# Up product of the routed expert tiles with the expert's weights as the stationary operand

## The reference

```python
xt = layernorm(x).reshape(2048, 512)
probs = softmax(xt @ W_router)                          # 16 routed experts, each token takes 2
rt_mid = gelu(einsum('th,ehd->ted', xt, Wrt_up))        # 512 -> 256
routed_out = einsum('ted,edh->th', rt_mid * gate, Wrt_down)   # 256 -> 512
```

## Time and profile before

| | us |
|---|---|
| median of three runs | 2106.89 |
| lowest and highest | 2105.78, 2107.63 |
| the profiled execution, its own time | 2111.85 |
| its span, first to last instruction | 2110.2 |
| stage of the routed tiles, first to last gelu start | 267.3 to 441.8 |

### The profile page before, as it was taken

How to read it: one execution, slowest core, us unless ns; L and a number is a source line. 1 busy time by engine, 2 the same in 40 slices (tenths; PEclk the granted TensorE clock), 3 DMA queues, 4 the chain that set the end, 5 groups by cost and what they waited for, 6 DMA issues and landing times. The chain is left out here.

```text
span 2110.2 us, 28970 instructions
## 1 busy us (share of the span) xinstructions
PE 1998.1 (95%) x9797; PEld 1654.6 (78%) x9801; DVE 1324.3 (63%) x2087; ACT 851.0 (40%) x1649; POOL 907.6 (43%) x802
## 2 busy tenths in 40 slices
PE   4989999957999999999999999999979999999999
PEld 4766788845888888887888888888867888888887
DVE  7985688867787676768676666666665333333333
ACT  4543299944444444444444444444432111111111
POOL 1100044434766767766666656666641122201200
PEclk9999999987999999999999999999989999999999
DMA  7350299964765666656555555555520010100002
GB/s 286 125 190 25 91 364 410 410 231 132 203 182 167 178 175 188 184 165 190 146 166 164 165 147 153 158 161 161 170 90 12 30 31 30 31 0 30 0 1 80
DMA packets 133759, 307.18 MB, mean 146 GB/s; under 512 B 15648, under 2 KB 17056, under 8 KB 133664
## 3 DMA queue, kind: packets, MB, share of 16 engines
q1 hardware_dynamic: 113600, 239.35, 36.7%
q0 software_dynamic: 20064, 66.60, 9.4%
HBM read 210.73 MB, written 95.16 MB: 145 GB/s over the span
## 5 line engine op out<-in xcount | busy, mean ns | idle before, releaser
L1482 POOL TENSOR_TENSOR t_pT_lo<-t_pT_raw,t_pT_hi 128x512 fp32r<-128x512 f32 x256 | 327.9, 1301 | 214.6 <-ACT t_pT_hi L1598 213.0
L1708 DVE TENSOR_REDUCE t_sums<-t_score 128x1 f32<-128x512 f32 x256 | 169.4, 687 | 128.8 <-PE t_score L52 128.4
L2084 DVE TENSOR_TENSOR f_lin<-f_lin,f_silu 128x512 f32<-128x512 f32 x64 | 44.7, 699 | 290.6 <-PE f_lin L52 290.6
L1613 ACT ACTIVATE t_probs<-t_score,t_sums 128x512 f32<-128x512 f32 x256 | 174.9, 683 | 84.1 <-DVE t_sums L1708 68.8
L1698 DVE STREAM_TRANSPOSE t_blocks<-t_probs 128x512 f32<-128x512 f32 x256 | 172.6, 693 | 23.9 <-ACT t_probs L1613 23.8
L1690 DVE SCALAR_TENSOR_TENSOR x_res<-t_out,t_sums,x_res 128x512 f32<-128x512 f32 x256 | 179.4, 740 | 7.4 <-PE t_out L52 7.4
L1598 ACT ACTIVATE t_pT_hi<-t_pT_raw 128x512 fp32r<-128x512 f32 x256 | 159.8, 625 | 3.9 <-DMA t_pT_raw<-turned_blocks 3.9
L2045 ACT ACTIVATE f_silu<-f_gate 128x512 f32<-128x512 f32 x64 | 38.3, 598 | 299.4 <-PE f_gate L52 299.4
L1592 ACT ACTIVATE t_o_hi<-t_o 128x512 fp32r<-128x512 f32 x64 | 38.3, 598 | 218.2 <-PE t_o L52 218.2
L1578 ACT ACTIVATE t_k_hi<-t_score 128x512 fp32r<-128x512 f32 x64 | 38.3, 598 | 204.6 <-PE t_score L52 204.6
L52 PE MATMUL t_score<-t_wv_hi,t_cT_hi 128*128 128x256 f32 x416 | 117.8, 283 | 0.8 <-ACT t_probs L1613 0.7
(11 more groups left out here) (351 smaller groups left out, 5953.0 us busy)
## 6 DMA issues: line engine op xcount, KB each, us to landing
turned_blocks<-t_blocks SPq DMA_DIRECT2D x256, 256.0 KB, 3.6
t_pT_raw<-turned_blocks SPq DMA_DIRECT2D x256, 256.0 KB, 4.2
e_up_raw<-in_L_ffn_Wrt_up_dram SPq DMA_DIRECT2D x47, 512.0 KB, 10.7
e_down_raw<-in_L_ffn_Wrt_down_dram SPq DMA_DIRECT2D x47, 512.0 KB, 10.1
outputs_by_expert<-e_y_out POOLq DMA_DIRECT2D x47, 256.0 KB, 5.9
wq_raw<-in_L_xattn_Wq_dram POOLq DMA_DIRECT2D x32, 256.0 KB, 4.5
wk_raw<-in_L_xattn_Wk_dram POOLq DMA_DIRECT2D x32, 256.0 KB, 2.9
wv_raw<-in_L_xattn_Wv_dram POOLq DMA_DIRECT2D x16, 512.0 KB, 5.0
```

The lines of the kernel that those rows point to most:

```text
L1482: pool.tensor_tensor(pT_lo[:, q], pT_raw[:, q], f32(pT_hi[:, q]), ALU.subtract).then_inc(p_ready, 1)
L1613: act.activation(probs[:, t % 2, :], score_bank[t][:, :], ACT.Exp, bias=neg_max[:, t:t + 1], accum_out=inv[:, p, t:t + 1]).then_inc(exp_re ...
L1708: dve.tensor_reduce(neg_max[:, t:t + 1], score_bank[t][:, :], AX.X, ALU.max, negate=True).then_inc(max_ready, 1)
L2084: dve.tensor_tensor(lin_bank[k][:, :], lin_bank[k][:, :], silu[:, k, :], ALU.mult).then_inc(mid_done, 1)
```

## The change

In the up product of a routed tile the operands change places. The weights become stationary, in two halves: half m takes the columns m, m+2, m+4, ... of the 256 (a step of two fp32 values between the columns that are loaded), and 128 columns of turned tokens move. The product comes out with middle values on the partitions and tokens along the row, in the layout that the down product wants. `turn_mid`, its semaphore and its two PSUM banks go. gelu is the same instruction on the same number of values; the high and low parts of the middle are now made from `gmid` in SBUF, and not from PSUM.

```diff
-        midT_bank, y_bank = [bank[7], bank[6]], bank[4:6]
+        y_bank = bank[4:6]
...
                 if n >= 2:
-                    act.wait_ge(gmid_turned, n - 1)
+                    act.wait_ge(midT_ready, n - 1)
                 act.activation(gmid[:, n % 2, :], mid_bank[n % 2][:, 0:DE], ACT.Gelu).then_inc(gmid_ready, 1)
 
-            def mid_turn_hi(n):
-                act.wait_ge(gmid_turned, n + 1)
+            def middle_hi(n):
+                act.wait_ge(gmid_ready, n + 1)
                 if n >= 2:
                     act.wait_ge(g_down_done, n - 1)
-                act.activation(midT_hi[:, n % 2], turned_over(midT_bank[n % 2])[:, 0:KE],
+                act.activation(midT_hi[:, n % 2], turned_over(gmid[:, n % 2]),
                                ACT.Copy).then_inc(midT_hi_ready, 1)
...
-            def mid_turn_lo(n):
+            def middle_lo(n):
                 dve.wait_ge(midT_hi_ready, n + 1)
-                dve.tensor_tensor(midT_lo[:, n % 2], turned_over(midT_bank[n % 2])[:, 0:KE], f32(midT_hi[:, n % 2]),
+                dve.tensor_tensor(midT_lo[:, n % 2], turned_over(gmid[:, n % 2]), f32(midT_hi[:, n % 2]),
                                   ALU.subtract).then_inc(midT_ready, 1)
...
-                three_pass(pe, mid_bank[r][:, 0:DE], lambda k: xgT_hi[:, r, k, :], lambda k: xgT_lo[:, r, k, :],
-                           lambda k: up_hi[:, r, k, :], lambda k: up_lo[:, r, k, :], KD).then_inc(g_up_done, 1)
-
-            def turn_mid(n):
-                pe.wait_ge(gmid_ready, n + 1)
...
-                by_row = gmid[:, r, :].rearrange("p (t k) -> p k t", k=KE)
-                for k in range(KE):
-                    ins = pe.transpose(midT_bank[r][:, k * P:(k + 1) * P], by_row[:, k, :], ident[:, :])
-                ins.then_inc(gmid_turned, 1)
+                for m in range(KE):
+                    ms = slice(m, DE, KE)
+                    ins = three_pass(pe, mid_bank[r][:, m * P:(m + 1) * P], lambda k: up_hi[:, r, k, ms],
+                                     lambda k: up_lo[:, r, k, ms], lambda k: xgT_hi[:, r, k, :],
+                                     lambda k: xgT_lo[:, r, k, :], KD)
+                ins.then_inc(g_up_done, 1)
...
                     turn(n + 2)
-                turn_mid(n)
                 if n + 1 < NSLOT:
                     g_up(n + 1)
                 g_down(n)
```

More of the change, by code:

```diff
@@ L682, in experts_phase @@
         gmid_ready = al.sem("gmid_ready")
-        gmid_turned = al.sem("gmid_turned")
         midT_hi_ready, midT_ready = al.sem("midT_hi_ready"), al.sem("midT_ready")
@@ L899, in _ @@
             for n in range(NSLOT):
-                mid_turn_hi(n)
+                middle_hi(n)
                 if n + 2 < NSLOT:
@@ L1107, in _ @@
             for n in range(NSLOT):
-                mid_turn_lo(n)
+                middle_lo(n)
                 if n + 2 < NSLOT:
```

## The result

The changed kernel took 2151.46 us (median of 2149.24 to 2152.03), the one before 2107.26 beside it: 1.0204 times, 95% interval 1.0191 to 1.0217, so +44.2 us where +46.5 was forecast. Its profiled execution took 2149.24 us, with a span of 2147.6.

What follows compares the result with a forecast made beforehand. DMA bounded the stage, TensorE just behind. With 24 up matmuls a TensorE tile takes 4.77 us for 3.79: 45.1 us over 46 tiles plus 1.4 at the start, +46.5 on 2106.9, so 2153 us; range 2138 to 2210.

Steps and rivals of the forecast that it cites:

- The bound: Routed-tile stage before the change: DMA sets the pace at 3.83 us a tile, TensorE 0.1 to 0.2 us behind.
- The saving: TensorE loses two transposes of the middle, 0.26 us, and a 0.08 us wait: 0.34 us a tile, not collected.
- The price of a short matmul: Up product: an fp32r matmul with 128 columns moving and its load costs 0.117 us, 24 for 12 a tile.
- the test of 0.22 against 0.28 us: Up matmul rows of 128 columns should last 0.22 us (columns at full rate) or 0.28 (at fp32's rate).
- The step: Up weight loads: skipping every second value costs something, 0.117 us a matmul; at 0.112 the total is 5 us less.
- rival (a): Up matmuls: step stretches the load, or loads and short matmuls don't overlap, 0.163 us each, +98 us, 2205; chance 0.14.
- The sum: TensorE tile: transposes 0.47, up 2.81 plus 0.09, down 1.40, together 4.77 us for 3.79; 46 tiles give 45.1 us.
- the start: First up product, ahead of the loop with nothing beside it: 1.4 us more.
- The rest: Program outside the stage: moving by more than a few us while the stage grows by 45 would make the prediction wrong.
- (b): Up matmuls: loads overlap each other, columns set 0.057 us each, DMA stays the pace, 0 to 2 us gained, 2106; chance 0.07.
- (c): Up matmuls: loads partly overlap, 0.083 us each, +8 us, 2115; chance 0.05.
- (d): Up matmuls: short fp32r runs at a rate below fp32's, over 0.2 us each, +150 us or more; chance 0.03.

Runs made afterwards that it cites:

- e4: Changed kernel with the up product of the kernel before (12 matmuls, 256 weight columns moving), middle not turned at all: 2108.3 us, 0.9996 of the kernel before.
- e5: Kernel before, with only half of each tile's down weights loaded from the fifth tile on: 2100.6 us, 0.9963 of the kernel before.
- e3: Kernel before, with the up product in 24 matmuls of 128 moving weight columns, tokens stationary, middle still turned: 2155.6 us, 1.0214 of the kernel before.
- e1: Changed kernel plus nine streams of 24 extra matmuls on TensorE behind the last down product, varying load, step, columns and type: ran once, 2168.6 us.
- e1 (9): Extra stream of 24 plain fp32 products added to the changed kernel, 128 weights loaded, 128 columns moving: 48 rows, 112 ns from start to start.
- e2: Changed kernel with the up weights' halves side by side (columns 0 to 127, 128 to 255), down weights loaded to fit: 2143.0 us, 1.0161 of the kernel before.
- stream (1): Extra fp32r matmuls added to the changed kernel, 128 weights loaded side by side, 128 columns moving: 112 ns from start to start.
- (2): Extra fp32r matmuls added to the changed kernel, 128 weights loaded with a step of two, 128 columns moving: 118 ns from start to start.
- e10: Changed kernel with 16 up loads, VectorE adding high and low token halves ahead of the weight splits, up-weight halves side by side: 2118.5 us, 1.0050 of the kernel before.
- e7: Changed kernel with half of each tile's down weights left out of the loads from the fifth tile on: 2149.6 us, 1.0194 of the kernel before.
- e1 (4): Extra fp32r matmuls added to the changed kernel, 64 weights loaded, 128 columns moving: 60 ns from start to start.
- 3 and 7: Extra fp32r streams added to the changed kernel, 128 weights loaded, 64 columns moving: side by side 112 ns, step of two 118 ns from start to start.

## Why the prediction was right

**The bound.** That DMA sets the pace and TensorE stands just behind it held: e4 and e5 show it from both sides.

**The saving.** 0.34 us of TensorE a tile was a little low. The turn of the earlier trace rows loses 0.81 - 0.39 = 0.42: 0.24 for the two transposes (e3), for which I had 0.26, and 0.18 for the wait, for which I had 0.08. The first transpose starts 0.08 late, and the second then starts 0.22 after it (343.60 and 343.82 in the trace), where two transposes in a stream stand 0.12 apart. The value of the saving, nothing, was right (e4).

**The price of a short matmul.** 0.117 us against 0.118 measured, and the reason was right: the load can't be hidden under 128 columns (e1). That it agrees to 1 ns is luck: the 0.117 came from another instruction, the tokens' transposes, and is their average with a first step of 0.11; their steady step in the trace is 0.120. One piece of evidence was misread, without harm: I took the plain fp32 rows for whole products, and e1 (9) shows that each row is half a product with a full load of its own. What I took from them stays, since one such row needs 0.43 us for 512 columns and so 0.107 for 128, and can't tell load from columns. And the test of 0.22 against 0.28 us for the matmul's duration would have spoken for the wrong theory: it was 0.28, because of the load.

**The step.** Right in sign and near in size: 118 against 112 ns (e1), 8 us (e2) where I said 5, and 7 before the run. But 206 against 141 ns was no measure of it, and rival (a)'s 0.163 us, which was worked out from it, had no ground. The transposes whose columns lie side by side, those with 141 ns, go start to start in (1.47 - 0.27) / 11 = 0.109 us:
```profile
185.77 1.47 PE L1159 MATMUL e_bank<-ident,e_xn 128*128 128x128 f32 x12
```
The stepped ones go in 0.120, so the 65 ns by which their loads' rows are longer cost 11 ns. In e1 the rows of fp32r loads differ by 5 ns (192 side by side in stream (1), 197 with the step in (2)) and the pace by 6. The Trainium skill ("SBUF — State Buffer", the note on cachelines) gives a step of two fp32 values full bandwidth; for weight loads these runs disagree, by 6 ns of 112 (e1). The Trainium skill's formula for a load, columns over 1.2 GHz ("TensorE: Matmul & The Clock Gate", LDWEIGHTS), gives an estimate of 107 ns for 128 columns, and e1 shows 112 from start to start.

**The sum.** The tile came out at 4.68 us on average and 4.72 in the list for 4.77: transposes 0.39 for 0.47, since the first up matmul starts 0.04 and not 0.12 us behind the start of the last transpose (in the earlier trace rows the middle's transposes stood in that place); first up matmul 0.15 for 0.20; the first down matmul 0.29 for 0.23. The stage grew by 215.3 - 174.5 = 40.8 us and the start by 1.0, for 45.1 and 1.4.

**The rest.** From the last gelu to the end of the span the two profiles have 1668.4 and 1664.0 us. I take that for scatter: in the nine kernels of e2 to e10 it lies between 1663.4 and 1667.5 (e1 adds to that part itself), with no order by kernel. The medians give +44.2 us and the stage with its later start +42; e7, whose stage is the same as the changed kernel's, is 41.4 over by the medians of its comparison. So some 42 us are explained, and 46.5 was 4 to 5 us too much for the stage; that the medians lie nearer to it isn't its merit.

**The rivals.** (a), 0.163 us: the changed kernel has 0.118, and no stream in e1 is above 0.120. (b) and (c), columns or half-overlapped loads, would need 0.057 to 0.083 with 128 weights; e1 has 60 only where fewer weights are loaded. The 81 ns that the Trainium skill ("TensorE: Matmul & The Clock Gate", Back-to-back issue gap) gives for 128 columns doesn't hold for fp32r: e1 (1) has 112. (d): dead by e1 (4).

## What to carry to other kernels

When the operands of a product change places, count the weight loads, not only the columns: the swap is free only while what moves is wide enough to hide each load. An fp32r load of 128 columns takes 112 ns. Under 256 moving columns (0.114 us) it was hidden; with 128 and with 64 it set the pace, in either orientation. Before saving work on an engine, ask whether it is the one that ends last: here the transposes stood behind DMA and were worth nothing, while the doubled loads made TensorE the last and were paid in full beyond DMA's pace. And a small instruction added to an engine's queue costs by its place: 75 us between two places of one line.

## What the runs showed of the hardware that I had not expected

- The row of a matmul of 64 columns lasts 279 ns behind a load of 128 columns, one of 128 columns 224 behind a load of 64 and 223 behind one of 32 (e1): a full load lengthens the row of the matmul that it holds up.
- In the streams of e1 fp32r matmuls keep 58 to 60 ns from start to start, with 64 as with 128 columns, with 64 as with 32 loaded; what sets that isn't shown.
- A plain fp32 product shows two loads and two matmuls, each 112 ns from start to start at 128 columns.
- A step of two fp32 values in the loaded weights costs 6 ns a load (e1, streams 1 and 2, and 3 and 7).
- A weight load's row can be 65 ns longer (206 against 141, transposes with and without a step) while the pace is 11 ns slower: read the price from start to start.
